# A transformer layer on one core: x requested ahead of the replication, output stores one slot later, the 704-column block scales in the next slot

## The chip, the core and the metric

The kernel runs on one core of a Trainium2 chip. The time is that of one execution on the device, in microseconds; the median of several runs counts. The engines are TensorE (PE, with its weight loads as PEld), VectorE (DVE), ScalarE (ACT), GpSimd (POOL) and SyncE (SP), which here only issues DMAs. Each runs its own list of instructions in order, and they wait for each other by semaphores.

## What is computed

```python
h = _layernorm(x) * (1 + ca) + sa
x = x + ga * attention(h)       # 16 heads of 16, relative bias, softmax, Wo
h = _layernorm(x) * (1 + cb) + sb
x = x + gb * ffn(h)             # gated, 256 -> 704 -> 256
# every operand of the ffn's three products goes through fp4_quant_dequant:
scale = jnp.max(jnp.abs(xb), axis=-1, keepdims=True) / 6.0   # blocks of 16
q = _GRID[jnp.searchsorted(_MID, jnp.abs(xb / scale))] * jnp.sign(xb / scale) * scale
```

x is 32 batches of 512 rows of 256 float32. ca, sa, ga, cb, sb, gb come from a small product per batch.

## The kernel before

The work runs in iterations n = -2 to 33; in steady state each covers one batch of attention, and other stages of its neighbours. An iteration has 16 slots s, each with four places j; a slot (s, j) is a place in the written order of every engine, not a time. `iterations` unrolls the first six and the last four and puts two (an even and an odd one) in a hardware loop between them. In each slot TensorE does scores and weighted sums of four heads of batch n, and for another batch the products whose row maxima VectorE takes (`maxima` and `reduce_max`, line 1078, on two PSUM banks: product k waits until row maximum k-2 is done). ScalarE takes the exp of two score banks at a time (line 824).

The feed-forward and the rest of the residual path go by tiles of 128 rows, four per batch, one for each group of four slots. With g = s // 4 and r = s % 4:

- x_mid has four tile buffers. One is loaded with x (SyncE, line 548), GpSimd adds a row to it at r = 0 (line 1328), VectorE adds the attention output at (1, 0) (`add_attention`, line 1148), then come the statistics, GpSimd's small operations of the second layer norm (lines 1342 to 1348) and ScalarE's application of them at (1, 2) (line 843). Some groups later VectorE adds the feed-forward output at (0, 3) (line 1196) and SyncE stores the buffer (line 561), after which it can be loaded again.
- hidden (128 x 704) is written by VectorE in slots r = 1 and 2. Its block scales are three VectorE operations (`block_scales`, lines 1113 to 1117), then GpSimd multiplies by the inverse (line 1362), ScalarE forms magic3 by a Square and an Identity (lines 852, 855), and in the next group's r = 0 GpSimd adds, subtracts and multiplies (lines 1333 to 1337). TensorE transposes the result, VectorE forms hq_l (line 1131), and TensorE does the "down" product in r = 3.

Queries and keys of batch n+2 are projected in slots 7 to 13, split in bfloat16 parts, stored to DRAM by SyncE in slots 10 and 14 (line 535), and read back by `replicate` in 12 copies for each half of the heads (line 521): half 0 in slot 11, half 1 after slot 15. x of batch n+2 is loaded to x_in (line 504) in slot 0; its statistics are taken by VectorE from place (2, 3) on (line 1088).

SyncE's list is strictly in order: whatever waits there holds back all DMAs behind it. All of them go through one hardware queue.

Of the kernel before, what the change touches and what calls it, by code (L numbers as in the profile page):

```python
# [34 lines left out]
H, HD = 16, 16  # L35
FF = 704
NT = S // P
# [81 lines left out]
def wait(eng, sem, value):  # L119

    if not (isinstance(value, int) and value <= 0):
        eng.wait_ge(sem, value)


def after(eng, steps, unit, name):
    wait(eng, steps.sem, steps.value(unit, name))
# [13 lines left out]
JOBS = job_table()  # L140
CHUNK_AT = {(1, 1): 0, (2, 0): 1, (2, 1): 2}

LN1_STATS = ((2, 3), (3, 0), (3, 1), (3, 3))
LN1_APPLY = ((4, 3), (5, 3))


# [1 line left out]
FIRST, LAST = -2, B + 1  # L148
# [114 lines left out]
def build(nc, x, wq, wk, wv, wo, bq, bk, bv, bo, rel, wg, wu, wd, c_t, wmod, cst, rows_dram, band_dram, parts_dram, out):  # L263
    with ExitStack() as ctx:
# [7 lines left out]
        q_rows = [sb(f"q_rows{i}", [P, H, S], BF16) for i in range(2)]  # L272
        k_rows = [sb(f"k_rows{i}", [P, H, S], BF16) for i in range(2)]
# [180 lines left out]
        def _(sp):  # L454
# [37 lines left out]
            def place_consts():  # L492

                sp.wait_ge(su_dve, SD["end"])
                sp.dma_start(q_rows[1][CR], ind[CR].unsqueeze(1).broadcast_to([P - ROWS_QK, H, S])
                             ).then_inc(consts_placed, 16)
                sp.dma_start(k_rows[1][CR], k_rows[0][CR]).then_inc(consts_placed, 16)
                sp.wait_ge(consts_placed, 48)
                sp.wait_ge(mod_stored, 16)

            def load_x(b):

                after(sp, a_act, b - 1, "h1b")
                sp.dma_start(x_in[:], x_v[:, bass.ds(b, 1), :, :].rearrange("p b t d -> p (b t) d")).then_inc(x_loaded, 16)
# [5 lines left out]
                             rows_dram[bass.ds(b, 1)].rearrange("b a d -> b (a d)").partition_broadcast(P)  # L510
                             .rearrange("p b n -> p (b n)")).then_inc(rows_loaded[par], 16)

            def replicate(it, half):


                wait(sp, scores_ready, 64 * it.n + 32 * (half + 1))
                for op, dst in ((0, q_rows[it.par]), (1, k_rows[it.par])):
                    wait(sp, parts_stored[2 * half + op], 16 * (it.n + 3))
                    src = parts_dram[it.par, half, op].rearrange("(h d) c n -> c d h n", d=HD)
                    for term, part in enumerate((TERMS_Q, TERMS_K)[op]):  # L520
                        sp.dma_start(dst[16 * term:16 * term + 16, 8 * half:8 * half + 8, :],  # L521
                                     src[part]).then_inc(replicated[half], 16)

            def emit(whole):
                it = whole
                n, par = it.n, it.par
                for s in range(16):
                    it = whole.fresh(sp, s)
                    n = it.n
                    if s in (10, 14) and it.has(2):  # L530
                        for p in ((0, 1) if s == 10 else (2, 3)):
                            after(sp, low_pool, 4 * (n + 2) + p, "low")

                            wait(sp, replicated[p // 2], 16 * N_REP * (n + 1))
                            sp.dma_start(parts_dram[par, p // 2, p % 2], parts[:, p % 2]).then_inc(parts_stored[p], 16)
                    if s == 11 and it.has(2):
                        replicate(it, 0)
                    if s == 0 and it.has(2) and (it.steady or n > FIRST + 1):
                        load_x(n + 2)
                    if s == 8 and not it.steady and n == FIRST:  # L540
                        load_x(n + 3)
                    if s == 12 and it.has(0):
                        load_rows(n, par)
                    if s % 4 == 0 and it.has_tile(s, -1):

                        t = s // 4
                        wait(sp, stored[t], 16 * (n - 1))
                        sp.dma_start(x_mid[:, t, :], x_v[:, bass.ds(n - 1, 1), t, :].rearrange("p b d -> p (b d)")
                                     ).then_inc(xres_loaded[t], 16)
                    if s in (3, 12):  # L550
                        half = 0 if s == 12 else 1
                        shift = 1 - half
                        if it.has(shift):
                            qr = q_rows[(par + shift) % 2]
                            after(sp, m_act, 2 * (n + shift) + half, "rows")
                            sp.dma_start(qr[ROW_MAX:ROW_MAX + 1, 8 * half:8 * half + 8, :].rearrange(
                                "p h (b q) -> p (h b) q", q=P), max_rows[:]).then_inc(max_placed[half], 16)
                    if s % 4 == 3 and it.has_tile(s, 2):
                        after(sp, f3_dve, it.tile(s, 2), "out")
                        tt = (s // 4 + NT - 3) % NT  # L560
                        sp.dma_start(out_v[:, bass.ds(it.tile(s, 2), 1), :].rearrange("p b d -> p (b d)"),
                                     x_mid[:, tt, :]).then_inc(stored[tt], 16)
                if it.has(2):
                    replicate(it, 1)
                if not it.steady and it.n == FIRST:
                    place_consts()

            iterations(sp, emit)
            for done in stored:
# [214 lines left out]
        def _(act):  # L784
# [25 lines left out]
            def emit(whole):  # L810
                it = whole
                n, par = it.n, it.par
                for s in range(16):
# [3 lines left out]
                    for j in range(4):  # L817
# [26 lines left out]
                        if (r, j) == (2, 3) and it.has_tile(s, 0):  # L844
                            u = it.tile(s, 0)
                            after(act, f1_pool, u, "xn")
                            A(magic2[:], ffn_in[:], ACT.Square, scale=ROOT).then_inc(f1_act.sem, 1)
                        if (r, j) == (3, 1) and it.has_tile(s, 1):
                            u = it.tile(s, 1)
                            after(act, f2_pool, u, "xn")  # L850
                            after(act, f3_pool, u - 1, "sub")
                            A(magic3[:], hidden[:, g % 2, :], ACT.Square, scale=ROOT).then_inc(f3_act.sem, 1)
                        if (r, j) == (3, 3) and it.has_tile(s, 1):
                            after(act, f3_act, it.tile(s, 1), "sq")
                            A(magic3[:], magic3[:], ACT.Identity, bias=floor[:]).then_inc(f3_act.sem, 1)
                        if (s, j) in MID_AT and it.has(2):
                            p = MID_AT.index((s, j))
# [90 lines left out]
        def _(dve):  # L948
# [249 lines left out]
            def emit(whole):  # L1198
                for s in range(16):
# [3 lines left out]
                    for j in range(4):  # L1203
# [25 lines left out]
                        if it.has_tile(s, 1):  # L1229
                            u = it.tile(s, 1)  # L1230
                            hid = hidden[:, g % 2, :]
                            if at == (2, 2):
                                after(dve, f2_dve, u, "h2")
                                after(dve, f3_pool, u - 1, "q")
                                block_scales(f2_dve, u, scale3[:], inv3[:], hid)
# [11 lines left out]
        def _(pool):  # L1247
# [54 lines left out]
            def emit(whole):  # L1302
                for s in range(16):
# [52 lines left out]
                            q.tensor_tensor(blocks(ffn_in[:]), blocks(ffn_in[:]), spread(inv2[:], D // BLK),  # L1356
                                            ALU.mult).then_inc(f1_pool.sem, 1)
                    low(it, s)
                    if r == 2 and it.has_tile(s, 1):
                        hid = hidden[:, g % 2, :]  # L1360
                        after(pool, f2_dve, it.tile(s, 1), "inv")
                        q.tensor_tensor(blocks(hid), blocks(hid), spread(inv3[:], FF // BLK),  # L1362
                                        ALU.mult).then_inc(f2_pool.sem, 1)
# [41 lines left out]
```

## Time and profile before

| | before |
|---|---|
| median of 3 runs | 3417.11 us (3414.52 to 3418.05) |
| profiled execution | 3417.14 us, of which span 3415.2 us |
| TensorE busy, granted clock | 3166.1 us (93%), 0.979 |
| VectorE, ScalarE, GpSimd busy | 83%, 62%, 50% |
| SyncE's store (line 561) waiting for VectorE's sum | 1712.4 us in 128 waits |
| SyncE's x_mid load waiting for the store | 227.2 us in 95 waits |
| x_in load, x_mid load, output store: median landing | 8.7, 2.1, 1.7 us |

The profiled execution equals the median of the runs. Its time is the span from the first to the last instruction and 1.9 us around it. A wait of SyncE costs nothing by itself; it sets when the DMAs behind it are issued. In the timelines below, a steady iteration is shown: slot 12 begins at about 1583.5 us, slot 13 at 1589.6, slot 14 at 1596.1, slot 15 at 1601.2, and the next iteration's slot 0 at 1608.3 (the first scores of each on TensorE), its slot 3 at 1625.3.

### The profile page before, as it was taken

To read this page: it belongs to the slowest core of one execution; us is meant where nothing else is said; L and a number is where in the kernel's file an instruction comes from. 1 tells how busy PE (TensorE), PEld (TensorE's weight loads), DVE (VectorE), ACT (ScalarE), POOL (GpSimd) and SP (SyncE) were. 2 spreads that over 40 slices of the span, in tenths; PEclk is the share of its full clock that TensorE was granted. 3 is DMA by queue.
4 is the path that set the end of the run, shared out by engine and by line. 5 is a ranking of instruction groups with operands and counts; after the bars stand their busy time and mean duration, and the time that the engine had idled before them with its cause. 6 is when DMAs were issued, how large, how long until landed. Compare 5 with 4: busy or idle time off the path is not lost.

```text
span 3415.2 us, 81836 instructions
## 1 busy us (share of the span) xinstructions
PE 3166.1 (93%) x22404; PEld 1887.6 (55%) x22404; DVE 2832.6 (83%) x9960; ACT 2123.3 (62%) x3389; POOL 1720.2 (50%) x2104
## 2 busy tenths in 40 slices
PE   4899999999999999999999999999999999999985
PEld 1345555555555555555555555565555555555555
DVE  6678888888888888888888888888888888888855
ACT  2566666666666666666666666666666666666652
POOL 3425555554545544545554455554455545555455
PEclk7899999999999999999999999999999999999997
DMA  8344442433443433443333443332444242344000
GB/s 198 63 75 78 83 80 59 75 62 62 81 80 64 72 59 63 81 81 68 71 60 59 81 80 66 73 62 57 80 82 76 62 72 58 70 82 74 22 24 13
DMA packets 200320, 239.85 MB, mean 70 GB/s; under 512 B 23600, under 2 KB 178640, under 8 KB 199808
## 3 DMA queue, kind: packets, MB, share of 16 engines
q1 hardware_dynamic: 199840, 234.06, 36.6%
q8 instruction: 227, 3.72, 0.5%
q14 instruction: 253, 2.07, 0.2%
HBM read 164.57 MB, written 67.31 MB: 68 GB/s over the span
## 4 chain that ended last, share of the span: by engine, by line
PE 64%; issue 9%; DMA 8%; DVE 7%; SPq 5%; ACT 4%; DVEq 1%; POOL 0%; ACTq 0%; POOLq 0%
PE ps_x L681 20%; PE ps_o L670 10%; PE rings L652 10%; PE rings L635 9%; DMA x_in<-in_x 7%; PE ps_x L709 6%; SPq L521 5%; PE rings L638 3%; ACT probs L824 2%; PE ps_x L727 1%; DVE scale L1113 1%; DVE row_max L1078 1%; PE ps_x L716 1%; PE ps_x L733 1%; DVE x_mid L1196 1%
## 5 line engine op out<-in xcount | busy, mean ns | idle before, releaser
L1078 DVE CUSTOM_DVE_ANT_0 rings<-rings,band_z 128x512 f32<-128x512 f32 x2048 | 1415.7, 697 | 178.9 <-issue 172.3
L824 ACT ACTIVATE probs<-rings 128x1024 f32<-128x1024 f32 x1024 | 1047.7, 1023 | 583.3 <-PE rings L638 567.7
L652 PE MATMUL rings<-k_rows,q_rows 120*128 120x512 bf16 x2048 | 789.8, 387 | 108.5 <-DVE row_max L1078 106.5
L635 PE MATMUL rings<-q_rows,k_rows 121*128 121x512 bf16 x2048 | 704.9, 384 | 59.4 <-issue 27.3
L638 PEld LDWEIGHTS rings<-rev,band_t 128*128 128x128 f16 x5632 | 410.7, 98 | 292.7 <-issue 3.5
L670 PE MATMUL ps_o<-probs,values 128*32 128x512 f32 x4096 | 551.2, 610 | 0.0
L652 PEld LDWEIGHTS rings<-k_rows,q_rows 120*128 120x128 bf16 x2048 | 197.2, 96 | 585.6 <-DVE row_max L1078 463.8
L638 PE MATMUL rings<-rev,band_t 128*128 128x64 f16 x5632 | 501.6, 192 | 0.0
L681 PE MATMUL ps_x<-w_gu_h,xq_h 128*128 128x512 f32 (+1 forms) x768 | 356.7, 464 | 1.6 <-DVE xq_l L1123 1.6
L1366 POOL TENSOR_TENSOR ffn_in<-ffn_in,scale 128x256 f32<-128x256 f32 x128 | 79.5, 621 | 438.9 <-DVE ffn_in L1167 438.9
L681 PE MATMUL ps_x<-w_gu_h,xq_l 128*128 128x512 f32 (+1 forms) x768 | 288.9, 376 | 0.0
L1078 DVE DVE_READ_ACCUMULATOR2_ANT row_max<- 128x1 f32 x2048 | 288.8, 141 | 0.0
L681 PE MATMUL ps_x<-w_gu_l,xq_h 128*128 128x512 f32 (+1 forms) x768 | 285.7, 372 | 0.0
L635 PEld LDWEIGHTS rings<-q_rows,k_rows 121*128 121x128 bf16 x2048 | 199.0, 97 | 154.9 <-issue 71.9
L1177 DVE SCALAR_TENSOR_TENSOR tanh<-tanh,ps_x 128x256 f32<-128x256 f32 (+1 forms) x384 | 152.7, 398 | 144.9 <-ACT tanh L934 139.3
L681 PE MATMUL ps_x<-w_dn_h,hq_h 128*128 128x256 f32 x768 | 239.3, 312 | 21.6 <-DVE hq_l L1131 21.6
L1362 POOL TENSOR_TENSOR hidden<-hidden,inv 128x704 f32<-128x704 f32 x128 | 177.5, 1386 | 135.9 <-DVE inv L1117 135.9
L1342 POOL TENSOR_TENSOR mean_var<-mean_var,pow_consts 128x1 f32<-128x1 f32 x128 | 24.4, 191 | 421.8 <-DVE mean_var L1159 421.8
L1356 POOL TENSOR_TENSOR ffn_in<-ffn_in,inv 128x256 f32<-128x256 f32 x128 | 79.4, 620 | 302.8 <-DVE inv L1117 302.8
L681 PE MATMUL ps_x<-w_dn_h,hq_l 128*128 128x256 f32 x768 | 221.3, 288 | 0.0
L681 PE MATMUL ps_x<-w_dn_l,hq_h 128*128 128x256 f32 x768 | 221.2, 288 | 0.0
L1292 POOL TENSOR_TENSOR proj<-proj,parts 128x512 f32<-128x512 f32 x128 | 153.3, 1198 | 106.3 <-ACT parts L897 106.3
(180 smaller groups left out, 6666.5 us busy)
## 6 DMA issues: line engine op xcount, KB each, us to landing
parts_dram<-parts SPq DMA_DIRECT2D x128, 384.0 KB, 2.3
q_rows<-parts_dram SPq DMA_DIRECT2D x384, 128.0 KB, 4.7
k_rows<-parts_dram SPq DMA_DIRECT2D x384, 128.0 KB, 7.8
mod_rows<-mod_rows_dram SPq DMA_DIRECT2D x32, 640.0 KB, 6.9
x_in<-in_x SPq DMA_DIRECT2D x32, 512.0 KB, 8.7
x_mid<-in_x SPq DMA_DIRECT2D x128, 128.0 KB, 2.1
out<-x_mid SPq DMA_DIRECT2D x128, 128.0 KB, 1.7
k_rows<-band_dram SPq DMA_DIRECT2D x2, 1024.0 KB, 9.4
```

The lines of the kernel that those rows point to most:

```text
L521: sp.dma_start(dst[16 * term:16 * term + 16, 8 * half:8 * half + 8, :], src[part]).then_inc(replicated[half], 16)
L635: mm(ps_s[:, bank, :], kr[0:ROW_MAX + 1, h, k0:k0 + P], qr[0:ROW_MAX + 1, h, :], start=True, stop=False)
L638: m = mm(ps_s[:, bank, k0 + w * HALF:k0 + (w + 1) * HALF], band_t[:, h, P - w * HALF:2 * P - w * HALF], rev[:, 0, 0:HALF], start=False, st ...
L652: mm(ps_m[:, bank, :], q_rows[par][0:ROW_MAX, h, j * P:(j + 1) * P], k_rows[par][0:ROW_MAX, h, :], start=True, stop=True).then_inc(mscores ...
L670: m = mm(ps_o[32 * j:32 * j + 32, :], values[:, par, kb, h * VW:h * VW + 32], prob(u, j), start=kb == 0, stop=kb == NT - 1)
L681: m = mm(out, left[a][:, dt, :], right[b][:, dt, columns], start=i == 0, stop=i == len(terms) - 1)
L709: m = mm(ps[:, :], w[:, dt, half * P:(half + 1) * P], h_t[:, dt, :], start=dt == 0, stop=dt == DT - 1)
L824: A(prob_pair(s, j), ps_s, ACT.Exp).then_inc(exp_done, 1)
L1078: v.tensor_tensor_reduce(ps, ps, band_z[:, bias:bias + S], 1.0, LOWEST, ALU.add, ALU.max, row_max[:, par, 4 * h + j:4 * h + j + 1]).then_i ...
L1177: v.scalar_tensor_tensor(tanh[:, c % 2, 0:w], tanh[:, c % 2, 0:w], 1.0, ps[:, 0:w], ALU.add, ALU.mult).then_inc(f2_dve.sem, 1)
L1292: q.tensor_tensor(pr, pr, parts[:, p % 2, 0, :], ALU.subtract).then_inc(rest_pool.sem, 1)
L1362: q.tensor_tensor(blocks(hid), blocks(hid), spread(inv3[:], FF // BLK), ALU.mult).then_inc(f2_pool.sem, 1)
```

## The change

x_in's load moves ahead of the replication of half 1, which itself moves from the end of an iteration to slot 0 of the next. The output store moves from slot 4g+3, where it waits for a sum of the following slot, to slot 4g+1 behind that sum. The x_mid load moves from slot 4g to slot 4g+3. The block scales of hidden move from place (2, 2) to (3, 0); GpSimd's product after them is written under r = 3 in place of r = 2; ScalarE's Square moves from (3, 1) to (3, 3), next to its Identity. Two statistics of the first layer norm move by a place or two.

```diff
-LN1_STATS = ((2, 3), (3, 0), (3, 1), (3, 3))
+LN1_STATS = ((2, 3), (3, 1), (3, 2), (3, 3))
...
-            def replicate(it, half):
+            def replicate(it, half, back):
...
+                n, par = it.n - back, (it.par + back) % 2
...
                     if s == 11 and it.has(2):
-                        replicate(it, 0)
+                        replicate(it, 0, 0)
                     if s == 0 and it.has(2) and (it.steady or n > FIRST + 1):
                         load_x(n + 2)
+                    if s == 0 and it.has(1):
+                        replicate(it, 1, 1)
...
-                    if s % 4 == 0 and it.has_tile(s, -1):
-
-                        t = s // 4
-                        wait(sp, stored[t], 16 * (n - 1))
-                        sp.dma_start(x_mid[:, t, :], x_v[:, bass.ds(n - 1, 1), t, :].rearrange("p b d -> p (b d)")
-                                     ).then_inc(xres_loaded[t], 16)
...
-                    if s % 4 == 3 and it.has_tile(s, 2):
-                        after(sp, f3_dve, it.tile(s, 2), "out")
-                        tt = (s // 4 + NT - 3) % NT
-                        sp.dma_start(out_v[:, bass.ds(it.tile(s, 2), 1), :].rearrange("p b d -> p (b d)"),
-                                     x_mid[:, tt, :]).then_inc(stored[tt], 16)
-                if it.has(2):
-                    replicate(it, 1)
...
+                    if s % 4 == 1 and it.has_tile(s, 3):
+                        after(sp, f3_dve, it.tile(s, 3), "out")
+                        sp.dma_start(out_v[:, bass.ds(it.tile(s, 3), 1), :].rearrange("p b d -> p (b d)"),
+                                     x_mid[:, s // 4, :]).then_inc(stored[s // 4], 16)
+                    if s % 4 == 3 and it.has_tile(s, -1):
+
+                        t = s // 4
+                        wait(sp, stored[t], 16 * (n - 1))
+                        sp.dma_start(x_mid[:, t, :], x_v[:, bass.ds(n - 1, 1), t, :].rearrange("p b d -> p (b d)")
+                                     ).then_inc(xres_loaded[t], 16)
...
-                        if (r, j) == (3, 1) and it.has_tile(s, 1):
+                        if (r, j) == (3, 3) and it.has_tile(s, 1):
...
-                            if at == (2, 2):
+                            if at == (3, 0):
                                 after(dve, f2_dve, u, "h2")
                                 after(dve, f3_pool, u - 1, "q")
                                 block_scales(f2_dve, u, scale3[:], inv3[:], hid)
...
-                    if r == 2 and it.has_tile(s, 1):
+                    if r == 3 and it.has_tile(s, 1):
```

SyncE's list from slot 7 to slot 12 of one iteration, before (the number behind `stored_` and the like is the buffer; low_pool says that a part is ready):

```order
L561 DMA out<-x_mid 128x256 [waits f3_dve]
L548 DMA x_mid<-in_x 128x256 [waits stored_2]
L535 DMA parts_dram<-parts 128x1536 [waits heads_0_7_replicated,low_pool] x2
L521 DMA q_rows1<-parts_dram 16x8x512 [waits parts_stored_0,scores_ready]
L521 DMA q_rows1<-parts_dram 16x8x512 x5
L521 DMA k_rows1<-parts_dram 16x8x512 [waits parts_stored_1]
L521 DMA k_rows1<-parts_dram 16x8x512 x5
L561 DMA out<-x_mid 128x256 [waits f3_dve]
L509 DMA mod_rows<-mod_rows_dram 128x1280 [waits f3_dve]
L548 DMA x_mid<-in_x 128x256 [waits stored_3]
L556 DMA q_rows0<-max_rows 1x32x128 [waits m_act]
```

and after, from the store of slot 9 to that of slot 13 (lines 521, 535, 548, 556 and 561 are now 522, 536, 565, 555 and 559):

```order
L559 DMA out<-x_mid 128x256 [waits f3_dve]
L536 DMA parts_dram<-parts 128x1536 [waits heads_0_7_replicated,low_pool] x2
L522 DMA q_rows1<-parts_dram 16x8x512 [waits parts_stored_0,scores_ready]
L522 DMA q_rows1<-parts_dram 16x8x512 x5
L522 DMA k_rows1<-parts_dram 16x8x512 [waits parts_stored_1]
L522 DMA k_rows1<-parts_dram 16x8x512 x5
L565 DMA x_mid<-in_x 128x256 [waits stored_2]
L509 DMA mod_rows<-mod_rows_dram 128x1280 [waits f3_dve]
L555 DMA q_rows0<-max_rows 1x32x128 [waits m_act]
L559 DMA out<-x_mid 128x256 [waits f3_dve]
```

The x_mid load of buffer 2 stood directly behind its store, ahead of the parts and the twelve copies; it now stands behind the twelve copies, and the output store left that place.

SyncE's list from the end of an iteration into the next, before:

```order
L561 DMA out<-x_mid 128x256 [waits f3_dve]
L521 DMA q_rows0<-parts_dram 16x8x512 [waits parts_stored_2,scores_ready]
L521 DMA q_rows0<-parts_dram 16x8x512 x5
L521 DMA k_rows0<-parts_dram 16x8x512 [waits parts_stored_3]
L521 DMA k_rows0<-parts_dram 16x8x512 x5
L504 DMA x_in<-in_x 128x4x256 [waits a_act]
L548 DMA x_mid<-in_x 128x256 [waits stored_0]
```

and after:

```order
L536 DMA parts_dram<-parts 128x1536 [waits heads_8_15_replicated,low_pool] x2
L565 DMA x_mid<-in_x 128x256 [waits stored_3]
L504 DMA x_in<-in_x 128x4x256 [waits a_act]
L522 DMA q_rows0<-parts_dram 16x8x512 [waits parts_stored_2,scores_ready]
L522 DMA q_rows0<-parts_dram 16x8x512 x5
L522 DMA k_rows0<-parts_dram 16x8x512 [waits parts_stored_3]
L522 DMA k_rows0<-parts_dram 16x8x512 x5
L559 DMA out<-x_mid 128x256 [waits f3_dve]
```

The x_in load has passed the twelve copies, and no output store stands before it.

VectorE's list from slot 14, place 2, on, before (L1078 is the row maximum, hq_l the low part of the transposed hidden):

```order
L1113 TENSOR_REDUCE scale3<-hidden 128x44 [waits f3_pool,f2_dve]
L1115 TENSOR_SCALAR scale3<-scale3 128x44 [waits f2_dve]
L1117 RECIPROCAL inv3<-scale3 128x44 [waits f2_dve]
L1131 TENSOR_TENSOR hq_l<-ps_x,hq_h 128x512 [waits f3_act,job_ready]
L1076 MEMSET wait_pad 128x1 [waits mscores_ready]
L1078 ISA rings,row_max<-rings,band_z 128x512
L1078 ISA row_max 128x1
L1131 TENSOR_TENSOR hq_l<-ps_x,hq_h 128x256 [waits f3_act,job_ready]
L1076 MEMSET wait_pad 128x1 [waits mscores_ready]
L1078 ISA rings,row_max<-rings,band_z 128x512
L1078 ISA row_max 128x1
L1076 MEMSET wait_pad 128x1 [waits mscores_ready]
```

and after, where these line numbers are one lower:

```order
L1130 TENSOR_TENSOR hq_l<-ps_x,hq_h 128x512 [waits f3_act,job_ready]
L1075 MEMSET wait_pad 128x1 [waits mscores_ready]
L1077 ISA rings,row_max<-rings,band_z 128x512
L1077 ISA row_max 128x1
L1130 TENSOR_TENSOR hq_l<-ps_x,hq_h 128x256 [waits f3_act,job_ready]
L1075 MEMSET wait_pad 128x1 [waits mscores_ready]
L1077 ISA rings,row_max<-rings,band_z 128x512
L1077 ISA row_max 128x1
L1112 TENSOR_REDUCE scale3<-hidden 128x44 [waits f3_pool,f2_dve]
L1114 TENSOR_SCALAR scale3<-scale3 128x44 [waits f2_dve]
L1116 RECIPROCAL inv3<-scale3 128x44 [waits f2_dve]
L1075 MEMSET wait_pad 128x1 [waits mscores_ready]
```

The three operations on the scales of hidden (128x44) come after both hq_l and two more row maxima. The order on GpSimd and TensorE is unchanged.

## Rows read from the trace of the kernel before

**Rows 1.** The page, busy time, share of the span and instructions of each engine

```profile
PE 3166.1 (93%) x22404; PEld 1887.6 (55%) x22404; DVE 2832.6 (83%) x9960; ACT 2123.3 (62%) x3389; POOL 1720.2 (50%) x2104
```

**Rows 2.** Waits of TensorE, 500 to 3050 us: us in total, times, longest

```profile
PE rings L652 <- DVE row_max L1078: 68.9, 50, 2.4
```

**Rows 3.** Timeline of TensorE: start, us, operation, idle time before it and its releaser

```profile
1593.79 0.38 PE L652 MATMUL rings<-k_rows,q_rows 120*128 120x512 bf16 x1
...
1599.26 0.38 PE L635 MATMUL rings<-q_rows,k_rows 121*128 121x512 bf16 x1
...
1604.70 0.39 PE L652 MATMUL rings<-k_rows,q_rows 120*128 120x512 bf16 x1 [1.49 <-DVE row_max L1078]
...
1631.31 0.39 PE L652 MATMUL rings<-k_rows,q_rows 120*128 120x512 bf16 x1 [1.49 <-DVE row_max L1078]
```

**Rows 4.** Timeline of VectorE

```profile
1590.49 1.37 DVE L1148 TENSOR_TENSOR x_mid<-tanh,x_mid 128x256 f32<-128x256 f32 x1
...
1601.63 0.88 DVE L1113 TENSOR_REDUCE scale<-hidden 128x44 f32<-128x704 f32 x1
...
1603.34 0.63 DVE L1131 TENSOR_TENSOR hq_l<-ps_x,hq_h 128x512 fp32r<-128x512 f32 x1
...
1629.82 0.43 DVE L1088 BATCH_NORM_STATS2 stats<-x_in 128x6 f32<-128x256 f32 x1 [1.58 <-DMA x_in<-in_x]
```

**Rows 5.** Waits of VectorE, 500 to 3050 us

```profile
DVE stats L1088 <- DMA x_in<-in_x: 33.8, 25, 2.4
```

**Rows 6.** Timeline of SyncE's queue, issues from slot 9 to the next slot 0

```profile
1566.11 0.33 SPq L548 DMA_DIRECT2D x_mid<-in_x  x1
...
1578.67 2.73 SPq L521 DMA_DIRECT2D q_rows<-parts_dram  x6
1581.45 2.80 SPq L521 DMA_DIRECT2D k_rows<-parts_dram  x6
1588.94 0.36 SPq L561 DMA_DIRECT2D out<-x_mid  x1
...
1594.67 0.34 SPq L548 DMA_DIRECT2D x_mid<-in_x  x1
...
1599.53 3.74 SPq L535 DMA_DIRECT2D parts_dram<-parts  x2
...
1620.60 0.41 SPq L504 DMA_DIRECT2D x_in<-in_x  x1
```

**Rows 7.** Timeline of ScalarE

```profile
1596.07 0.60 ACT L843 ACTIVATE ffn_in<-x_mid,shift,rstd 128x256 f32<-128x256 f32 x1 [0.98 <-POOL shift L1348]
...
1597.36 1.01 ACT L824 ACTIVATE probs<-rings 128x1024 f32<-128x1024 f32 x1
...
1606.69 0.87 ACT L855 ACTIVATE magic<-magic,pow_consts 128x704 bf16<-128x704 bf16 x1
1609.23 1.02 ACT L824 ACTIVATE probs<-rings 128x1024 f32<-128x1024 f32 x1 [1.68 <-PE rings L638]
```

**Rows 8.** Landing of the x_mid load issued at 1566.11, nothing before it

```profile
DMA to landing us min/median/max: 2.0/2.0/2.0
```

**Rows 9.** Timeline of GpSimd, slots 12 to 16

```profile
1584.67 0.74 POOL L1328 TENSOR_TENSOR x_mid<-x_mid,mod_rows 128x256 f32<-128x256 f32 x1
...
1590.41 1.17 POOL L1292 TENSOR_TENSOR proj<-proj,parts 128x512 f32<-128x512 f32 x1 [0.39 <-ACT parts L897]
1594.71 0.19 POOL L1342 TENSOR_TENSOR mean_var<-mean_var,pow_consts 128x1 f32<-128x1 f32 x1 [3.14 <-DVE mean_var L1159]
...
1608.30 0.72 POOL L1328 TENSOR_TENSOR x_mid<-x_mid,mod_rows 128x256 f32<-128x256 f32 x1
```

**Rows 10.** Landing of the two last k_rows copies, issued 1583.3 and 1583.8

```profile
DMA to landing us min/median/max: 9.8/10.0/10.3
```

**Rows 11.** Landing of the output store issued at 1588.94

```profile
DMA to landing us min/median/max: 5.6/5.6/5.6
```

**Rows 12.** Landing of the x_mid load issued at 1621.27, behind x_in

```profile
DMA to landing us min/median/max: 9.5/9.5/9.5
```

More of the change, by code:

```diff
@@ L511, in load_rows @@
                              .rearrange("p b n -> p (b n)")).then_inc(rows_loaded[par], 16)
-            def replicate(it, half):
[L516 to L519, printed above, removed]
+            def replicate(it, half, back):
+                n, par = it.n - back, (it.par + back) % 2
+                wait(sp, scores_ready, 64 * n + 32 * (half + 1))
+                for op, dst in ((0, q_rows[par]), (1, k_rows[par])):
+                    wait(sp, parts_stored[2 * half + op], 16 * it.n + 16 * (3 - back))
+                    src = parts_dram[par, half, op].rearrange("(h d) c n -> c d h n", d=HD)
                     for term, part in enumerate((TERMS_Q, TERMS_K)[op]):
@@ L536, in emit @@
                     if s == 11 and it.has(2):
-                        replicate(it, 0)
+                        replicate(it, 0, 0)
                     if s == 0 and it.has(2) and (it.steady or n > FIRST + 1):
                         load_x(n + 2)
+                    if s == 0 and it.has(1):
+                        replicate(it, 1, 1)
+                    if s == 0 and not it.steady and n == FIRST + 1:
+                        place_consts()
                     if s == 8 and not it.steady and n == FIRST:
@@ L557, in emit @@
                                 "p h (b q) -> p (h b) q", q=P), max_rows[:]).then_inc(max_placed[half], 16)
-                    if s % 4 == 3 and it.has_tile(s, 2):
-                        after(sp, f3_dve, it.tile(s, 2), "out")
-                        tt = (s // 4 + NT - 3) % NT
-                        sp.dma_start(out_v[:, bass.ds(it.tile(s, 2), 1), :].rearrange("p b d -> p (b d)"),
-                                     x_mid[:, tt, :]).then_inc(stored[tt], 16)
-                if it.has(2):
-                    replicate(it, 1)
-                if not it.steady and it.n == FIRST:
-                    place_consts()
+                    if s % 4 == 1 and it.has_tile(s, 3):
[7 more added lines that the diff above has]
+                                     ).then_inc(xres_loaded[t], 16)
             iterations(sp, emit)
@@ L852, in emit @@
                             A(magic3[:], hidden[:, g % 2, :], ACT.Square, scale=ROOT).then_inc(f3_act.sem, 1)
-                        if (r, j) == (3, 3) and it.has_tile(s, 1):
-                            after(act, f3_act, it.tile(s, 1), "sq")
+                            after(act, f3_act, u, "sq")
                             A(magic3[:], magic3[:], ACT.Identity, bias=floor[:]).then_inc(f3_act.sem, 1)
```

## The prediction, made before the changed kernel was run

> **What bounds the kernel now.** I read the share of busy time first: TensorE is busy for 93% of the span, VectorE for 83% [rows 1]. A stretch of 25 iterations in the steady part takes 2550 us (500 to 3050), 102 us each, so the question is what TensorE's few idle moments are. Its waits there [rows 2] name one large releaser, VectorE's row maximum (line 1078): 68.9 us in 50 waits, two in each iteration, 1.38 us each. The timeline of TensorE puts them in slots 3 and 15 [rows 3]. In slot 15 VectorE had the three operations on the 704-column scales in front of that row maximum, from 1601.63 to 1603.34, 1.7 us [rows 4]. In slot 3 it had those and a wait for x_in as well: 33.8 us in 25 waits, 1.35 us per iteration [rows 5], one of them before the statistics at 1629.82 [rows 4]. So the change goes at the right two stalls, and together they are worth at most 2.8 us per iteration. I then read SyncE's queue [rows 6], because three of the four edits reorder it, and the timelines of GpSimd, VectorE and ScalarE in slots 12 to 15.
>
> **x ahead of the replication.** Before, SyncE stops at the output store of slot 15 until VectorE's sum in the next slot 0, then issues 12 copies, and only then x_in, at 1620.60. Its landing is what VectorE waits for in slot 3. Now x_in stands right behind slot 15's small load. The two parts stores end on SyncE at 1599.53 + 3.74 = 1603.3 [rows 6], so x_in is issued some 17 us earlier, and its wait is gone. The replication of half 1 now waits only for the last scores and is not needed before slot 10: free. What is late next in slot 3 is VectorE's own work, and the moved scales take 1.7 us out of that place too. I price slot 3 at the whole stall, -1.4 us.
>
> **Block scales of 704 columns.** The same three operations, 1.7 us, run after two row maxima and two hq_l instead of before them. Slot 15's stall of 1.49 [rows 3] would vanish by itself. The chain behind them is GpSimd's multiply, then ScalarE's Square and Identity; these now stand together in front of the next slot's exp. In the trace ScalarE's last of them ends at 1606.69 + 0.87 = 1607.56 and the exp starts at 1609.23 after waiting 1.68 for TensorE [rows 7]. That idle time is the cover. The new chain ends about as late as TensorE's scores come, late by up to 1 us where the cover is short, and TensorE has some slack behind an exp (1599.26 - 1598.37 = 0.9 us one slot earlier [rows 3, 7]). I price it at 0 to +0.5, value +0.1.
>
> **Outputs and x_mid loads.** This is the part that I think decides. x_mid has four tile buffers; each is stored, loaded with x for a later tile, and then read by GpSimd's first addition of a group (line 1328). Before, the reload was issued in the slot divisible by four, four slots ahead of its reader. Now the store stands in slot 4g+1 and the reload in slot 4g+3, one slot ahead of its reader in 4g+4.
> - Slots 3 and 7: the queue is empty, a load then lands in 2.0 us [rows 8], and a slot is over 6 us. Free.
> - Slot 15: issued behind the parts stores at about 1603.4, it lands by about 1606 to 1606.5; GpSimd's addition is at 1608.30 [rows 9]. Free, with some 2 us to spare.
> - Slot 11: the reload now stands behind `replicate(it, 0, 0)`, 12 copies of 128 KB each. Before, it went out at 1566.11, ahead of them [rows 6]. Now it goes out when the last copy has been issued, 1581.45 + 2.80 = 1584.25, so about 1584.4.
>
> When does it land? The last k_rows copies, issued until 1583.8, land 10.3 us later, at 1594.1 [rows 10]. The output store issued at 1588.94 behind the same copies needed 5.6 us and landed at 1594.5 [rows 11], where a free queue gives about 2 [rows 8]; the x_mid load of slot 0, which stands behind replication and x_in, takes 9.5 [rows 12]. So the new load lands between 1594.1 and 1594.5; I take 1594.3. The Trainium skill, "DMA: Bandwidth & Descriptors", section "Queues, rings and completion order", says that each DMA engine takes descriptors in ring order, but that completion is not first-in first-out per issuing engine. By the second half of that rule a small late load could land early and nothing would be lost (the first rival); by the first half it stands in line. The trace agrees with the first half.
>
> GpSimd starts that addition at 1584.67 today [rows 9]. So it will stand for 9.6 us and end at 1594.3 + 0.7 = 1595.0. Queued behind it on GpSimd are the three hidden operations and the rest of p3: from 1584.67 to 1590.41 + 1.17 = 1591.58 it takes 6.9 us, 0.39 of that a wait, so 6.5 of work. Its next step, the small operations of the second layer norm (1594.71 today, released by VectorE), can then start at 1594.3 + 6.5 = 1600.8, 6.1 us late. VectorE's sum at 1590.49 [rows 4] waits until 1595.0, 4.5 late; that brings the statistics at 1599.2, before 1600.8, so GpSimd's queue is what ends last. ScalarE waits in order for the shift: line 843 goes from 1596.07 to 1602.2, and the exp behind it from 1597.36 to 1603.5, ending at 1604.5 instead of 1598.4 [rows 7]. TensorE's next scores are at 1599.26 [rows 3], 0.9 us of slack, so they come at 1604.5: +5.2. (By VectorE's delay alone TensorE would stand at 1593.79, waiting for the row maximum, some 3.3 us; this lies inside the 5.2.)
>
> Slot 15 pays a part back. VectorE runs 6.1 late through slot 14 (it waits for ScalarE's tanh), less the 1.7 us of scales: its row maximum is 4.4 later than today, and TensorE, which must first take the row maximum and the weighted sums that stand before it, is about +4.6 there. The 1.49 stall is thus gone but only 0.6 of it is won.
>
> **Sum.** Slots 12 to 15: +4.6; held exp +0.1; slot 3: -1.4. That is +3.3 us per iteration. The late load exists where a tile is loaded in slot 11 and half 0 is replicated there, n = 1 to 29: 29 x 3.3 = +96 us. The last iterations have stalls and no late load: about -4. The profiled execution took 3417.1 us (span 3415.2 and 1.9 around it), equal to the median, so 3417 + 92 = 3509; I say 3510.
> Bounds per iteration: below, only VectorE's delay reaches TensorE (3.3) and both stalls are won (2.8): +0.5, +15 us. Above, the full 6.1 and nothing won: +177 us. My value lies between, nearer the rows of ScalarE, which are in-order and have no cover.
>
> **Rivals.**
> - *The load is not late* (it lands early, or some earlier issue covers it). For it: the sentence above on completion. Against it: the three landings [rows 10 to 12]. It would leave the gains: 29 x 2.8 less 0.1 to 0.5 held, -67 to -80 us, 3337 to 3350. Chance 0.06.
> - *Late but swallowed*: GpSimd is idle half the time, and the delay is absorbed so that loss equals gain. It needs ScalarE to be late by no more than 3.7 us at line 843 (0.9 of slack and 2.8 of gains), that is a landing before about 1592. 3405 to 3425. Chance 0.05.
> - *Late and nothing given back*: GpSimd is late 6.1, the hidden chain is late too, and the scales in slot 15 now hold the exp in each group. TensorE loses 5.2 and up to 1 more, gains only in slot 3: +4.8 x 29 = +140, 3557, up to 3590. For it: the chain GpSimd, ScalarE has no slack left once GpSimd lags. Chance 0.17.
> - *The held exp alone costs*: in every group's last slot Square and Identity push exp back 1 us: 4 x 1 x 30 = +120 without a late load, less 80 won, 3450. Against it: ScalarE idles 1.68 us before that exp [rows 7]. It decides if GpSimd's product ends over 1.7 us later than ScalarE's exp. Chance 0.05.
>
> **How the numbers follow.** My forecast, 3480 to 3545, has 0.67. Eight times in ten lies within 3465 to 3565: the forecast and the nearer half of the third rival. A measurement of this kernel tells about 0.2%, 7 us, from no change. Slower by more: 0.67 + 0.17 + 0.05 and the upper edge of the second case, 0.90; within: 0.03; faster: 0.07.
>
> **What would show it.** In the changed profile GpSimd's first addition (line 1328, or its shifted number) in slot 12 shows a wait of about 9 us per iteration for DMA x_mid, some 270 us in all, and that x_mid load takes about 10 us to land. ScalarE's wait for the shift of the second layer norm grows by about 6 us once per iteration. VectorE's wait for x_in is gone, TensorE's stall in slot 3 too. TensorE idles 3 us in slot 13 and more in slot 14. I am wrong if the x_mid load of slot 11 lands within 3 us, or if GpSimd waits there and ScalarE's exp of slot 14 still comes on time.

## The result, and the profile after

| | before | changed |
|---|---|---|
| median | 3415.82 us (4 runs) | 3558.59 us (4 runs, 3547.36 to 3566.31) |
| ratio | | 1.0417 (95%: 1.0387 to 1.0448) |
| profiled execution | 3417.14 us | 3547.36 us |
| TensorE busy, granted clock | 3166.1 us, 0.979 | 3230.7 us, 0.959 |

The kernel became 4.2% slower, 143 us; 93 had been forecast. The changed kernel's profiled execution is its fastest, 11 us below the median. Line numbers of the changed kernel are one lower in the compute part (1327 for 1328, 1147 for 1148), and x_mid's load is line 565.

The totals of GpSimd, ScalarE and TensorE in 25 iterations (530 to 3180 us): us in total, times, longest.

```profile
POOL x_mid L1327 <- DMA x_mid<-in_x: 230.9, 25, 9.6
```

```profile
ACT ffn_in L843 <- POOL shift L1347: 208.5, 98, 7.1
```

```profile
PE rings L652 <- DVE row_max L1077: 97.9, 69, 3.7
PE rings L635 <- issue: 55.9, 12, 6.2
```

GpSimd waits for the x_mid load in every iteration, 9.2 us each; before, it never did. The numbers of before are from its own 25 iterations, 500 to 3050 us. ScalarE's wait for the shift grew from 78.0 us to 208.5. TensorE's wait for the row maximum grew from 68.9 us [rows 2]. The last line is the one that I had not looked at: "issue" (a wait for nothing that the profile shows) in front of the scores, 12 times, once each time the hardware loop branches back. Before, it was 27.3 us in 12.

Now one iteration. SyncE's queue from the copies of slot 11 to those of the next slot 0:

```profile
1636.51 2.73 SPq L522 DMA_DIRECT2D q_rows<-parts_dram  x6
1639.29 2.81 SPq L522 DMA_DIRECT2D k_rows<-parts_dram  x6
1642.38 0.36 SPq L565 DMA_DIRECT2D x_mid<-in_x  x1
...
1667.28 0.34 SPq L565 DMA_DIRECT2D x_mid<-in_x  x1
1667.95 0.39 SPq L504 DMA_DIRECT2D x_in<-in_x  x1
1668.56 2.70 SPq L522 DMA_DIRECT2D q_rows<-parts_dram  x6
1671.30 2.79 SPq L522 DMA_DIRECT2D k_rows<-parts_dram  x6
```

and the landing of the load issued at 1642.38:

```profile
DMA to landing us min/median/max: 9.4/9.4/9.4
```

Against [rows 6] the load now follows the last copy by 0.3 us, and lands 9.4 us later instead of 2.0 [rows 8]. x_in is issued at 1667.95, 0.6 us ahead of the other twelve copies. The timelines of GpSimd, VectorE, ScalarE and TensorE (start, duration, operation, idle time before it); this iteration lies 57.8 us behind the one shown before, by the first exp of slot 12:

```profile
1651.92 0.72 POOL L1327 TENSOR_TENSOR x_mid<-x_mid,mod_rows 128x256 f32<-128x256 f32 x1 [9.24 <-DMA x_mid<-in_x]
...
1657.19 1.16 POOL L1291 TENSOR_TENSOR proj<-proj,parts 128x512 f32<-128x512 f32 x1
1658.32 0.19 POOL L1341 TENSOR_TENSOR mean_var<-mean_var,pow_consts 128x1 f32<-128x1 f32 x1
```

```profile
1652.78 1.61 DVE L1147 TENSOR_TENSOR x_mid<-tanh,x_mid 128x256 f32<-128x256 f32 x1 [4.50 <-POOL x_mid L1327]
```

```profile
1659.67 0.60 ACT L843 ACTIVATE ffn_in<-x_mid,shift,rstd 128x256 f32<-128x256 f32 x1 [6.76 <-POOL shift L1347]
...
1660.97 1.01 ACT L824 ACTIVATE probs<-rings 128x1024 f32<-128x1024 f32 x1
```

```profile
1655.13 0.48 PE L652 MATMUL rings<-k_rows,q_rows 120*128 120x512 bf16 x1 [3.35 <-DVE row_max L1077]
1656.54 0.61 PE L652 MATMUL rings<-k_rows,q_rows 120*128 120x512 bf16 x1
1659.16 0.39 PE L635 MATMUL rings<-q_rows,k_rows 121*128 121x512 bf16 x1
...
1662.36 0.38 PE L635 MATMUL rings<-q_rows,k_rows 121*128 121x512 bf16 x1
...
1667.09 0.39 PE L635 MATMUL rings<-q_rows,k_rows 121*128 121x512 bf16 x1
```

Take 57.8 off and set them beside [rows 3, 4, 7, 9]: the second layer norm starts 5.8 us late on GpSimd (1658.32 against 1594.71), line 843 5.8 late, the scores of slot 14 at place 2 5.3 late (1662.36 against 1599.26). The second row of TensorE's shows something else: 0.61 us for the same product that takes 0.38. The view of stretches (us, TensorE busy, granted clock, DMA) says why:

```profile
1654.00:1655.00 1.00, 0.00 (x0) 1.00 0.00 0
1655.00:1656.00 1.00, 0.87 (x4) 0.65 0.00 0
1656.00:1657.00 1.00, 0.92 (x5) 0.50 0.00 0
1657.00:1658.00 1.00, 1.00 (x4) 0.50 0.00 0
1658.00:1659.00 1.00, 1.00 (x4) 0.65 0.06 16
1659.00:1660.00 1.00, 1.00 (x12) 1.00 0.00 0
```

After standing 3.35 us TensorE goes on at 0.5, that is 1.2 GHz, for some 3.5 us. From the product that had waited to slot 14's first scores it takes 4.03 us (1655.13 to 1659.16), against 2.27 before (1593.79 [rows 3] to 1596.06).

**Where the time went, by groups of four slots.** I took the time on TensorE from each group's first transpose of context to the next group's, and averaged between the first and the last of the 12 times at which the hardware loop branches back (11 or 12 groups in each column of groups 3 and 0). Group 3 is slots 12 to 15. The loop holds two iterations, so every second group 3 ends at the loop's back edge; the others are called clear. Group 0 is split in the same way, by the group 3 before it. The kernels e1 to e12 are the experiments below; there is no e5 and no e8.

| kernel | group 3, clear | group 0 after it | group 3, back edge | group 0 after it | group 1 | group 2 | per iteration |
|---|---|---|---|---|---|---|---|
| before | 24.8 | 26.0 | 27.3 | 26.0 | 25.0 | 24.7 | 101.8 |
| changed | 29.0 | 24.3 | 34.2 | 25.5 | 25.0 | 24.7 | 106.2 |
| e1 | 23.2 | 24.3 | 29.1 | 25.5 | 25.0 | 24.7 | 100.7 |
| e2 | 23.2 | 26.3 | 27.0 | 26.5 | 25.4 | 24.7 | 101.7 |
| e3 | 30.9 | 23.9 | 35.6 | 25.8 | 25.0 | 24.7 | 107.9 |
| e4 | 30.7 | 26.0 | 33.2 | 25.6 | 25.0 | 24.7 | 107.5 |
| e6 | 23.2 | 24.3 | 28.4 | 25.5 | 25.0 | 24.7 | 100.4 |
| e7 | 23.2 | 24.3 | 29.5 | 26.2 | 25.0 | 24.7 | 101.3 |
| e9 | 23.2 | 24.3 | 27.2 | 25.3 | 25.0 | 24.7 | 99.7 |
| e10 | 26.1 | 24.3 | 31.6 | 25.4 | 25.0 | 24.7 | 103.4 |
| e11 | 24.8 | 23.9 | 27.3 | 24.8 | 25.0 | 24.7 | 100.1 |
| e12 | 29.0 | 24.3 | 33.2 | 24.9 | 25.0 | 24.7 | 105.4 |

Groups 1 and 2 do not move, but for group 1 of e2. From before to changed, the clear group 3 lost 4.2 us and the group 0 after it won 1.7; the group 3 with the back edge lost 6.8 and the group 0 after it won 0.5. That is 2.5 us for an iteration without the back edge and 6.3 for one with it, 4.4 on average where 3.3 had been forecast.

### The profile page after: what moved, and what is told of

Same layout as the page of the kernel before. It is cut to its first block, busy times and chain, and to the rows that moved or that the text cites. A ratio compares the mean times of both kernels' runs of the same rounds, so it can differ in the third digit from the quotient of the medians.

```text
span 3545.5 us, 81862 instructions
## 1 busy us (share of the span) xinstructions
PE 3230.7 (91%) x22404; PEld 1913.3 (54%) x22404; DVE 2815.6 (79%) x9960; ACT 2146.0 (61%) x3389; POOL 1723.1 (49%) x2104
## 4 chain that ended last, share of the span: by engine, by line
issue 38%; POOL 31%; PE 10%; DMA 9%; SPq 5%; DVE 3%; ACT 2%; POOLq 2%; DVEq 0%; ACTq 0%
DMA x_mid<-in_x 8%; POOL hidden L1334 5%; POOL hidden L1332 4%; SPq L522 4%; POOL parts L1298 3%; PE ps_x L681 3%; POOL hidden L1361 3%; POOL hidden L1336 2%; POOL ffn_in L1349 2%; POOL proj L1291 2%; POOL rstd L1344 2%; PE rings L635 2%; POOL x_mid L1327 2%; PE ps_o L670 2%; POOLq L122 1%
## 5 line engine op out<-in xcount | busy, mean ns | idle before, releaser
L652 PE MATMUL rings<-k_rows,q_rows 120*128 120x512 bf16 x2048 | 803.2, 393 | 141.0 <-DVE row_max L1077 138.1
L681 PE MATMUL ps_x<-w_gu_h,xq_h 128*128 128x512 f32 (+1 forms) x768 | 369.6, 481 | 1.1 <-DVE xq_l L1122 1.1
L681 PE MATMUL ps_x<-w_gu_h,xq_l 128*128 128x512 f32 (+1 forms) x768 | 297.2, 387 | 0.0
L681 PE MATMUL ps_x<-w_gu_l,xq_h 128*128 128x512 f32 (+1 forms) x768 | 296.5, 386 | 0.0
L1147 DVE TENSOR_TENSOR x_mid<-tanh,x_mid 128x256 f32<-128x256 f32 x128 | 142.3, 1111 | 135.5 <-POOL x_mid L1327 130.6
L843 ACT ACTIVATE ffn_in<-x_mid,shift,rstd 128x256 f32<-128x256 f32 x128 | 76.9, 601 | 277.7 <-POOL shift L1347 254.9
L1327 POOL TENSOR_TENSOR x_mid<-x_mid,mod_rows 128x256 f32<-128x256 f32 x128 | 93.9, 734 | 266.7 <-DMA x_mid<-in_x 266.6
```

The lines of the kernel that those rows point to most:

```text
L652: mm(ps_m[:, bank, :], q_rows[par][0:ROW_MAX, h, j * P:(j + 1) * P], k_rows[par][0:ROW_MAX, h, :], start=True, stop=True).then_inc(mscores ...
L681: m = mm(out, left[a][:, dt, :], right[b][:, dt, columns], start=i == 0, stop=i == len(terms) - 1)
L1147: v.tensor_tensor(x_mid[:, t, :], gated, x_mid[:, t, :], ALU.add).then_inc(f1_dve.sem, 1)
L1327: q.tensor_tensor(x_mid[:, t, :], x_mid[:, t, :], mod_rows[:, rp, 1, :], ALU.add).then_inc(f1_pool.sem, 1)
```

## Experiments

**e1: the late load undone.** The x_mid load of slot 11 stands ahead of the parts stores; all else is the changed kernel.

```diff
+                    if s == 10 and it.has_tile(s, -1):
+                        t = s // 4
+                        wait(sp, stored[t], 16 * (n - 1))
+                        sp.dma_start(x_mid[:, t, :], ...).then_inc(xres_loaded[t], 16)
...
-                    if s % 4 == 3 and it.has_tile(s, -1):
+                    if s in (3, 7, 15) and it.has_tile(s, -1):
```

> The changed kernel, with one DMA moved: the x_mid load of buffer 2 stands in slot 10 ahead of the parts stores, so ahead of the twelve copies. My theory (this one late load is what costs): GpSimd's wait for x_mid (9.2 us per iteration) falls to none, ScalarE's wait of 6.8 us in slot 13 falls to 1, and the time falls from 3558 by about 5.3 us x 29 = 154 to about 3400; the gains in slots 3 and 15 then show and it ends below the kernel before (3370 to 3405). Rival (the scales' new place and the moved replication cost, the late load only lies beside it): it stays above 3500.

Measured 3386.20 us (4 runs), ratio to before 0.991 (0.9878 to 0.9942): 172 us less than the changed kernel, by the place of one DMA. GpSimd's wait for x_mid is gone from the list of its waits. The theory stands; the price was 5.9 us in each of 29 iterations, not 5.3 (5.6 by the two profiled executions, of which the changed kernel's lies 11 us below its median).

**e2: the scales' new place alone.** Before, with the compute edits of the change; GpSimd's product stays under r = 2, where it has the same place in GpSimd's order.

```diff
-LN1_STATS = ((2, 3), (3, 0), (3, 1), (3, 3))
+LN1_STATS = ((2, 3), (3, 1), (3, 2), (3, 3))
...
-                            if at == (2, 2):
+                            if at == (3, 0):
...
-                        if (r, j) == (3, 1) and it.has_tile(s, 1):
+                        if (r, j) == (3, 3) and it.has_tile(s, 1):
```

> The kernel before with the compute part of the change alone (block scales, Square, the two statistics), the DMA order as before. My theory: slot 15's stall of 1.5 us goes, 1.2 us of it is won, slot 3 keeps its wait for x_in and most of its stall; -35 to -45 us, 3375 to 3380. Rival (the held exp costs in every group): 3420 or more.

Measured 3410.79 us (10 runs), ratio 0.9984 (0.9965 to 1.0002): no change that can be told, and a miss for both. VectorE and TensorE from 500 to 3050 us:

```profile
DVE stats L1087 <- DMA x_in<-in_x: 61.8, 25, 3.3
```

```profile
PE rings L635 <- issue: 39.4, 12, 3.7
PE rings L652 <- DVE row_max L1077: 31.0, 25, 2.1
```

Slot 15's stall is gone (25 waits are left, the ones of slot 3), and the clear group 3 is 1.6 us shorter. But what VectorE wins ahead of slot 3 it stands waiting for x_in (61.8 us against 33.8 [rows 5]), and at the back edge TensorE stands 3.3 us where it stood 2.3, so that the group 3 there is only 0.3 us shorter. Groups 0 and 1 grew by 0.3 to 0.5 us each; no pair of kernels here takes that apart.

**e3 and e4: the queue's order alone, and the late load alone.** e3 has the changed SyncE list over the compute part of before. e4 is before with one DMA moved:

```diff
                     if s == 11 and it.has(2):
                         replicate(it, 0)
+                    if s == 11 and it.has_tile(s, -1):
+                        ... the x_mid load of buffer s // 4
...
-                    if s % 4 == 0 and it.has_tile(s, -1):
+                    if s in (0, 4, 12) and it.has_tile(s, -1):
```

> The kernel before with the DMA order of the changed one, the compute part as before. My theory: the late load costs 5.3 us per iteration here too, slot 3 gains 1.5, slot 15 keeps its stall or hides it under the delay: 3545 to 3590, not below the changed kernel by more than 15. Rival (the scales' place is a good part of the loss): 3480 or less.

> The kernel before with one DMA moved: the x_mid load of buffer 2 goes from slot 8 to behind the copies of slot 11. Nothing else changes; x_in and the replication of half 1 stay. My theory: GpSimd waits about 9 us per iteration for x_mid, +4.6 us x 29 = +133, 3530 to 3560. If the time before is 3416 and this gives much more than that, slot 15's stall is not hidden under the delay. Rival (GpSimd's delay is swallowed, the loss comes from elsewhere): under 3440.

Measured 3591.68 us, ratio 1.0517 (1.048 to 1.0554), and 3588.08 us, ratio 1.05 (1.0461 to 1.0539). e3 came out 2 us above the range expected and e4 28 us above. e4 gave +169 us against a kernel before of 3418.93 us in that session, more than the 133 expected: 5.8 us per iteration, in group 3 by 5.9 (clear) and 5.8 (back edge). As its text allowed for, slot 15's stall isn't hidden under the delay but comes on top:

```profile
1577.70 0.39 PE L658 MATMUL rings<-k_rows,q_rows 120*128 120x512 bf16 x1 [1.49 <-DVE row_max L1084]
```

169 here and 172 in e1 are the same price from both sides. e3 holds two things more. It differs from the changed kernel by the scales' place alone and is 33 us slower: with the late load there, the new place takes 2.0 us off the clear group 3 and 1.5 off the other. And it differs from e4 by the other queue edits alone, which together cost 4 us: its two groups 0 are 2.1 us shorter and 0.2 longer, and its group 3 with the back edge is 2.5 us longer, where TensorE stops 4.2 us in place of 2.2.

**e7 and e10: how late is too late.** The changed kernel with that load put in the middle of the twelve copies, after six (e7) and after nine (e10).

```diff
                 for op, dst in ((0, q_rows[par]), (1, k_rows[par])):
+                    if op == 1 and half == 0 and it.has_tile(11, -1):
+                        ... the x_mid load of buffer 2
...
-                    if s % 4 == 3 and it.has_tile(s, -1):
+                    if (s in (3, 7, 15) or s == 11 and not it.has(2)) and it.has_tile(s, -1):
```

> The changed kernel with the late load of slot 11 issued after six of the twelve copies. It should land about 6 us after its issue at some 1581.5 on the old time axis, 1587.5, so GpSimd waits 3 us, inside the 3.1 it otherwise waits for VectorE. Theory (the loss is GpSimd's delay less its slack): nearly the whole loss is gone, 3385 to 3400. Rival (loss in proportion to the wait): 3558 - 172 x 6/9 = 3443.

> The changed kernel with the late load issued after nine of the twelve copies: lands about 7.7 us after an issue at 1582.8, 1590.5; GpSimd waits 6 us, less 3.1 of slack leaves ScalarE 2.8 late, less TensorE's 0.9 leaves 1.9 us x 29 = 55: 3435 to 3450. Rival (loss in proportion to the wait, 6 of 9.2): 3500.

Measured 3398.68 us (7 runs), ratio 0.994 (0.9918 to 0.9961), and 3472.46 us, ratio 1.0157 (1.012 to 1.0194). GpSimd's waits, 500 to 3050 us, after six copies:

```profile
POOL x_mid L1331 <- DMA x_mid<-in_x: 80.5, 25, 3.4
```

and after nine:

```profile
POOL x_mid L1331 <- DMA x_mid<-in_x: 152.1, 24, 6.5
```

Against e1 the waits of 3.2, 6.3 and 9.2 us cost 12, 86 and 172 us in 29 iterations, 0.4, 3.0 and 5.9 us each. From 6.3 to 9.2 each microsecond of waiting costs one microsecond, and the line through them meets zero at 3.3 to 3.4. That is near GpSimd's own slack, 3.14 us of waiting for VectorE [rows 9]. The test of the line is e7: its clear group 3 is as long as that of e1, so the wait of 3.2 us costs nothing there, and its 12 us lie at the back edges alone. The rival of a loss in proportion (3443 and 3500) is out. e10 came out 22 us above the range expected: I took off TensorE's 0.9 us of slack on top, 26 us in 29 iterations, and it isn't there.

**e6 and e9: what lies in flight at the back edge.** e6 is e1 with the replication of half 1 moved behind the output store of slot 1; e9 moves x_in there too. The diff is that of e9 against e1.

```diff
-                    if s == 0 and it.has(2) and (it.steady or n > FIRST + 1):
-                        load_x(n + 2)
-                    if s == 0 and it.has(1):
-                        replicate(it, 1, 1)
...
+                    if s == 1 and it.has(2) and (it.steady or n > FIRST + 1):
+                        load_x(n + 2)
+                    if s == 1 and it.has(1):
+                        replicate(it, 1, 1)
```

> The previous experiment's kernel e1 (late load undone) with the replication of half 1 moved from slot 0 to slot 1, behind the output store, so that its twelve copies are not in flight when the engines take the loop's back edge; x_in stays ahead. Theory (copies in flight lengthen TensorE's stop at the back edge, 5.0 us each in e1 against 2.3 before): the stop falls to about 3.3, as in the scales-only kernel, time 3386 - 13 x 1.7..3 = 3350 to 3365. Rival (the stop is longer only because TensorE comes there earlier): 3380 to 3390.

> As e6, and the x_in load too stands in slot 1 behind the store, ahead of the replication: nothing large is in flight at the back edge, and x_in still has 10 us until its statistics and lands in 5 to 6. Theory (copies in flight): at or up to 10 us below e6. Rival (the fetch does not care about the queue): as e1, 3386.

Measured 3379.08 us, ratio 0.9881 (0.9845 to 0.9917), and 3362.11 us, ratio 0.983 (0.9794 to 0.9866). TensorE's stop at the back edge, 500 to 3050 us, in e1, in e6 and in e9:

```profile
PE rings L640 <- issue: 60.2, 12, 5.4
```

```profile
PE rings L640 <- issue: 51.6, 12, 4.8
```

```profile
PE rings L640 <- issue: 39.0, 12, 3.5
```

5.0, 4.3 and 3.3 us a pass, with copies and x_in, x_in alone, and nothing large in flight. e6 missed its range (3350 to 3365) and came out 1 us below its rival's; x_in alone already costs most of the longer stop. e9 speaks against that rival, and fell by 17 us where at most 10 were expected. e9 stops as long as e2, which has the same compute part and the old queue, so of the growth from 2.3 to 5.0 one microsecond comes with the compute part and 1.7 are the DMAs. e3 against e4, with the old compute part, gives 2.0 for the DMAs.

The trace also shows what TensorE waits for. Engines fetch their instructions by DMA; the page of the kernel before has two queues of that kind, in 3415 us:

```profile
q8 instruction: 227, 3.72, 0.5%
q14 instruction: 253, 2.07, 0.2%
```

(packets, MB, share of 16 engines). During one stop in e1, 2089.65 to 2094.57 us, the queues moved

```profile
q1 hardware_dynamic: 1281, 1.20, 100.2%
q8 instruction: 1, 0.02, 1.7%
```

and during one in e9, 2076.01 to 2079.16:

```profile
q8 instruction: 1, 0.02, 1.9%
q14 instruction: 2, 0.02, 1.9%
```

The last packet of q8, 16 KB, before TensorE goes on has its own time in the packed trace. Medians of the 12 back edges, in us from the beginning of the stop:

| kernel | packet begins | takes | has landed | TensorE goes on |
|---|---|---|---|---|
| before | -1.1 | 1.4 | 0.2 | 2.1 |
| e11 | -1.1 | 1.2 | 0.2 | 2.0 |
| e9 | 0.4 | 1.1 | 1.5 | 3.3 |
| e6 | 1.3 | 1.1 | 2.5 | 4.2 |
| e1 | 1.5 | 1.6 | 3.1 | 5.0 |
| changed | 1.4 | 1.2 | 2.6 | 4.5 |

In all twelve kernels TensorE goes on 1.8 to 2.0 us (median) after that packet has landed. With x_in in flight the packet begins 0.9 us later, with the copies behind it 1.1 us, and it takes up to 0.5 us longer. The new compute part does not delay the packet; it lets TensorE stop about 1.5 us earlier before it. That q8 is TensorE's own queue is inferred from this constant distance; the trace does not name its engine. Behind such a stop comes the lower clock, here in e1, where the first product takes 0.60 us:

```profile
2094.57 0.60 PE L640 MATMUL rings<-q_rows,k_rows 121*128 121x512 bf16 x1 [4.92 <-issue]
```

**e12: the same with the late load kept.** The changed kernel with x_in and the replication in slot 1.

> The changed kernel, its late load of slot 11 kept, with x_in and the replication of half 1 in slot 1 behind the store. Theory (copies in flight at the back edge cost the same here as in e1 against e9): TensorE's stop at the back edge falls from 4.6 to some 3.3 us, 3558 - 24 = 3530 to 3540. Rival (under the late load TensorE comes later anyway, so the stop is hidden): 3550 to 3565.

Measured 3528.05 us, ratio 1.033 (1.0308 to 1.0352): 30 us below the changed kernel, 2 us under the range expected. In the changed kernel the stop is 50.8 us in 11 back edges; here, in 12:

```profile
PE rings L635 <- issue: 40.6, 12, 3.7
```

**e11: what the scales are worth when x_in is in time.** e9's queue with the compute part of before.

> The kernel e9 (best DMA order so far) with the compute part of the kernel before: block scales at (2, 2), Square at (3, 1). It asks what the scales' new place is worth where x_in is in time. Theory (worth its slot-15 stall of 1.5 us in each iteration, of which the back edge takes back 1 us in every second one; slot 3 needs no scales move once x_in is there): 3362 + 1.3 x 32 - 13 = 3390 to 3400. Rival (the scales' place is worth nothing, as the run of it alone gave): 3362 to 3370.

Measured 3370.02 us, ratio 0.9868 (0.9846 to 0.9889). The scales' new place is worth 8 us here, not 30, and even the 8 are not clear of noise: the interval of this ratio overlaps that of e9. The rival was right. Group 0 is even 0.4 to 0.5 us shorter with the old place, and group 3 is 1.5 longer, but only clear of the back edge. TensorE's waits for the row maximum, 500 to 3050 us:

```profile
PE rings L657 <- DVE row_max L1083: 37.1, 25, 1.5
```

They are the 25 of slot 15. Those of slot 3 are gone: x_in's timeliness alone took the whole stall out of it. With the late load in the kernel the scales' place is worth 33 us (e3 against changed), so their worth depends on the rest.

## Why the prediction was right, and what it lacked

Direction, cause and the range (3465 to 3565) held; the central value was 3510 against 3558.6, near the upper end. One way from the kernel before to the changed one goes by e11, e9 and e1:

| part | kernels | us |
|---|---|---|
| x_in and the other queue edits, clear of the back edge | e11 against before | -44 |
| block scales later | e9 against e11 | -8 |
| x_in and replication at the back edge | e1 against e9 | +24 |
| x_mid load of slot 11 behind the copies | changed against e1 | +172 |
| sum | | +144 |

Each step begins where the last one ends, so the sum must come out near 143 and proves nothing. What checks a part is the same edit made elsewhere. The late load is steady: 169 in e4. The back edge gives 30 between e12 and changed. The scales are not: -33 between e3 and changed. Along that other way the parts are +169 (e4), +4 (e3, all other queue edits) and -33 (scales). The kernel before itself differed by up to 4.5 us between sessions, so a difference of a few microseconds says nothing.

- **The late load.** "Between 1594.1 and 1594.5", 9.6 us of standing on GpSimd: the row says 9.24. Six and a half microseconds queued behind it on GpSimd: right, 6.4 from 1651.92 to 1658.32. ScalarE 6.1 late, TensorE 5.2: measured 5.8 and 5.3. The way there was not quite mine. I let ScalarE's exp end last. It ended at 1661.98, and the scores followed at 1662.36 without a wait in the profile, 3.20 us after those of place 0, as before. TensorE was late by itself: 3.35 us for VectorE's row maximum, which I had called contained in the 5.2, and then 1.8 us because its clock was at half. Two paths ended within 0.4 us of each other, so the 5.2 came out partly by luck.
- **Slots 12 to 15, +4.6 and +0.1.** The clear group 3 grew by 4.2. Of slot 15's stall more was won than the 0.6 that I gave it: TensorE was 5.3 late in slot 14 and the group 4.2. Here the term was right; with the back edge the same group grew by 6.8.
- **Slot 3, -1.4.** TensorE's stall there is gone, as forecast, but by x_in alone; I had named the scales as a second cause, and with x_in in time they add nothing there. Group 0 won 1.7 us behind a clear group 3 and only 0.5 behind the back edge.
- **Replication of half 1: "free".** This is the step that failed. I checked when the copies are needed and not what else happens when they are in flight: they now stand in slot 0 at the loop's back edge, where TensorE's stop was in the trace all along. Together with x_in this costs 24 to 30 us. The other part is that slot 15's won stall is hardly collected where the back edge follows, in every second iteration of the loop (e2: 0.3 us there, 1.6 elsewhere). In groups 3 and 0 together an iteration with the back edge grew by 6.3 where 3.3 was forecast, a clear one by 2.5. That makes about 30 of the 50 us that were missed. Of the rest, 11 us is the distance of the changed kernel's median from the profiled execution in which these groups were measured, and some 9 us lie in the iterations outside the loop.
- **The rivals.** The load is late in every iteration, so the first is out. "Late but swallowed" needed a landing before about 1592 on the old axis; e7 shows that it is true for a landing some 6 us earlier. "Late and nothing given back" (3557) comes out at the right time for a wrong reason: slot 3's gain was there, and the scales gave 33 us back against e3. The held exp, where x_in is in time, costs at most the 0.4 to 0.5 us by which group 0 is longer in e9 than in e11.
- The Trainium skill's rule that descriptors are taken in ring order ("DMA: Bandwidth & Descriptors", "Queues, rings and completion order") agrees with the runs: 9.4 us behind twelve copies, and GpSimd's waits of 3.2 and 6.3 us behind six and nine.

The fastest kernel of the study is e9: 3362.1 us, 1.7% below the kernel before, with every edit of the change kept in substance, the x_mid load of slot 11 ahead of the parts stores, and x_in and the replication of half 1 behind the store of slot 1.

## What to carry to other kernels

When a DMA moves in a queue, price it by what stands before it and by its reader's slack, not by its own size: the same 128 KB load cost 12 us of the kernel's time behind six of twelve copies and 170 behind all twelve. Look for the reader's engine first, since all that is queued behind the reader is late as well. And look at what a moved transfer newly overlaps, loop branches included, even where nobody needs its data soon: at a branch it can stand beside the fetch of the engines' instructions.

## What the runs showed of the hardware

TensorE's granted clock fell to 0.5 (1.2 GHz) after it had stood 3.35 us in the changed kernel, and the same 512-column product took 0.61 instead of 0.38 us; about 3.5 us later it was back at 1.0. After the 1.49 us stall of slot 15 in the kernel before [rows 3] the product took 0.39. At the loop's back edge TensorE stops 2.1 to 2.3 us with the old compute part and nothing large in flight (e11, before), 3.3 with the new one (e9), and 5.0 in e1, where about 1 MB of x_in and the copies moves during the stop. In every kernel it goes on 1.8 to 2.0 us after a 16 KB packet of the instruction queue q8 has landed. A 128 KB load issued 0.3 us behind twelve copies of 128 KB in the same queue landed after 9.4 us, with nothing before it after 2.0.
